# Cross-attention on one core: one reciprocal instruction for two steps' denominators, and a new order of work on all engines

## What is computed

```
xn  = (input - mean) * rsqrt(var + 1e-5) * gamma + beta      # mean and var over the whole sample
q   = Wq @ xn + bq        -> 8 heads of 256 x 64
k,v = Wkv @ context + bkv -> 8 heads of 256 x 64
att = softmax(q k^T / 8)  # 256 x 256 for each head
y   = att @ v
out = input + Wo @ y + bo
```

## Time and profile before

| | us |
|---|---|
| median of 3 runs | 728.08 |
| lowest, highest | 727.77, 731.11 |
| the profiled execution, own time | 729.69 |
| its span, first to last instruction | 727.9 |
| busy DVE, PE, ACT, POOL | 676.4, 670.9, 620.0, 566.5 |
| mean granted clock of TensorE | 0.982 |
| one period of the loop (two samples) | 21.36 and 21.50 in turn |

### The profile page before, as it was taken

One profiled execution on the slowest core, in us unless ns is written; L12 is line 12 of the kernel. 1 busy time (PEld: TensorE's weight loads), 2 busy tenths in 40 slices (PEclk: granted clock), 3 DMA queues, 4 the chain that ended last, 5 costly groups with the idle time before them and its releaser, 6 DMA issues.

```text
span 727.9 us, 29934 instructions
## 1 busy us (share of the span) xinstructions
PE 670.9 (92%) x11204; PEld 445.4 (61%) x11204; DVE 676.4 (93%) x1124; ACT 620.0 (85%) x2248; POOL 566.5 (78%) x360
## 2 busy tenths in 40 slices
PE   5789999999999999999999999999999999899986
PEld 4556666666666656666665666666566666566564
DVE  1599999999999999999999999999999999999992
ACT  2579888899988889988888998888898888899882
POOL 2478888787888878888887888888788888778872
PEclk9789999999999999999999999999999999999997
DMA  6112222222222222222222222222222222222110
GB/s 123 26 53 74 72 57 65 77 70 70 70 72 62 58 69 70 70 74 60 61 67 70 70 70 70 65 58 69 70 70 72 65 66 56 74 73 60 43 47 23
DMA packets 74814, 47.56 MB, mean 65 GB/s; under 512 B 33748, under 2 KB 74708, under 8 KB 74772
## 3 DMA queue, kind: packets, MB, share of 16 engines
q1 hardware_dynamic: 72848, 46.59, 23.9%
q10 hardware_dynamic: 1924, 0.40, 0.3%
HBM read 25.96 MB, written 4.19 MB: 41 GB/s over the span
## 4 chain that ended last, share of the span: by engine, by line
PE 61%; DVE 16%; SPq 9%; issue 7%; ACT 4%; DMA 2%; DVEq 0%; ACTq 0%
PE z L399 30%; PE fill L365 24%; DVE neg_max L536 7%; SPq L290 6%; DVE probs_t L549 6%; PE z L410 4%; ACT probs L481 4%; PE z L424 1%; DVE y L592 1%; PE z L377 1%; DVE spread L580 1%; SPq L253 1%; SPq L242 1%; DMA x_res<-in_x 1%; DMA wv<-in_L_xattn_Wkv 1%
## 5 line engine op out<-in xcount | busy, mean ns | idle before, releaser
L637 POOL TENSOR_TENSOR probs<-probs,recip 128x1024 f32<-128x1024 f32 x256 | 482.1, 1893 | 127.3 <-DVE recip L542 126.3
L481 ACT ACTIVATE probs<-fill,neg_max 128x256 f32<-128x256 f32 x1024 | 472.7, 487 | 76.5 <-DVE neg_max L536 73.1
L536 DVE TENSOR_REDUCE neg_max<-fill 128x4 f32<-128x1024 f32 x256 | 307.8, 1202 | 15.9 <-PE fill L365 14.6
L365 PE MATMUL fill<-c,t 64*128 64x256 f32 x2048 | 290.1, 404 | 32.5 <-ACT probs L481 27.7
L549 DVE STREAM_TRANSPOSE probs_t<-probs 128x1024 f32<-128x1024 f32 x256 | 310.5, 1222 | 3.0 <-POOL probs L637 0.9
L365 PEld LDWEIGHTS fill<-c,t 64*128 64x128 f32 x2048 | 187.4, 189 | 123.6 <-ACT probs L481 88.7
L399 PE MATMUL z<-probs_t,ctx_keys 32*64 32x256 f32 x8192 | 253.1, 380 | 0.8 <-DVE y L592 0.7
L481 ACT ACTIVATION_READ_ACCUMULATOR probs<-fill,neg_max 128x1 f32 x1024 | 224.5, 219 | 0.0
L399 PEld LDWEIGHTS z<-probs_t,ctx_keys 32*64 32x64 f32 x8192 | 175.1, 131 | 64.9 <-issue 35.0
L490 ACT ACTIVATE t<-z,d_col 128x512 f32<-128x512 f32 x128 | 88.5, 740 | 7.4 <-PE z L377 7.4
L497 ACT COPY z_sb<-z 128x1024 f32<-128x1024 f32 x64 | 61.9, 1032 | 7.8 <-PE z L399 7.8
(11 more groups left out here) (38 smaller groups left out, 108.0 us busy)
## 6 DMA issues: line engine op xcount, KB each, us to landing
ctx_keys<-ctx_turned SPq DMA_DIRECT2D x512, 32.0 KB, 1.8
x<-in_x SPq DMA_DIRECT2D x64, 128.0 KB, 2.8
c<-in_ctx SPq DMA_DIRECT2D x64, 128.0 KB, 2.7
ctx_rows<-in_ctx SPq DMA_DIRECT2D x128, 32.0 KB, 1.8
x_res<-in_x SPq DMA_DIRECT2D x32, 128.0 KB, 2.2
out<-y SPq DMA_DIRECT2D x32, 128.0 KB, 1.8
wq<-in_L_xattn_Wq ACTq DMA_DIRECT2D x2, 128.0 KB
wv<-in_L_xattn_Wkv SPq DMA_DIRECT2D x2, 128.0 KB
```

Source lines behind the costliest of these rows:

```text
L365: mm = pe.matmul(banks[:, o, K * qt:K * qt + K], t[p][r:r + 64, hp, s, 128 * qt:128 * qt + 128], c2[p][r:r + 64, s, :], start=True, stop=True)
L481: ins = act.activation(probs[:, k % SLOTS, g, :], bank[:, K * qt:K * qt + K], ACT.Exp, bias=neg_max[:, k, g:g + 1], accum_out=denom[:, k, ...
L536: dve.tensor_reduce(neg_max[:, k, :], fill[k % PAIRS_OF_BANKS][:, :, :].rearrange("p o (t k) -> p (o t) k", t=QT), AX.X, ALU.max, negate=T ...
L637: pool.tensor_tensor(p, p, recip[:, k, :].unsqueeze(2).broadcast_to([128, 2 * QT, K]), ALU.mult).then_inc(probs_ready, 1)
```

## The change

Two things are done together. First, the denominators of steps 2i and 2i+1 are inverted by one instruction over 128 x 8, four times a pair in place of eight times 128 x 4. It waits for the exponentials of both steps, and the divides of both steps wait for it:

```
-            def reciprocal(pair, k):
-                wait(dve, exp_ready, pair.count(UNITS, 2 * k + 2))
-                dve.reciprocal(recip[:, k, :], denom[:, k, :]).then_inc(recip_ready, 1)
+            def reciprocals(pair, i):
+
+                wait(dve, exp_ready, pair.count(UNITS, 4 * i + 4))
+                dve.reciprocal(recip[:, 2 * i:2 * i + 2, :], denom[:, 2 * i:2 * i + 2, :]).then_inc(recip_ready, 1)
...
             def divide(pair, k):
-                wait(pool, recip_ready, pair.count(STEPS, k + 1))
+                wait(pool, recip_ready, pair.count(STEPS // 2, k // 2 + 1))
```

Second, the tables of all engines are replaced:

```
-PE_ORDER = (at('scores', 0.00, 1.20, 3.50, 5.03, 7.25, 10.15, 10.92, 13.57)
-            + at('mix', 18.05, 18.82, 20.27, 21.80, 22.56, 24.01, 24.77, 25.46) + at('project_out', 30.26)
-            + at('project_in', -4.39, -3.70) + at('mean', -16.17) + at('var', -14.90))
-ACT_ORDER = (at('exp', 1.93, 3.30, 5.47, 7.40, 9.19, 12.09, 13.89, 15.69) + at('t', -2.54, -0.74, 1.06, 1.48)
-             + at('z', 26.56, 27.29))
-DVE_ORDER = (at('weights', -2.59, 1.02) + at('max', 0.97, 2.25, 4.51, 6.44, 8.23, 11.13, 12.83, 14.59)
-             + at('recip', 4.45, 6.38, 8.14, 9.07, 10.85, 13.67, 15.43, 18.19)
-             + at('turn', 7.28, 9.13, 9.99, 11.97, 13.73, 15.49, 19.59, 21.35) + at('moments', -28.92)
-             + at('mean_var', -25.79) + at('spread', -15.34) + at('sample_var', -14.19)
-             + at('turn_context', 1.89) + at('result', 32.35))
-POOL_ORDER = (at('divide', 4.65, 6.75, 8.33, 9.74, 11.15, 13.87, 15.63, 18.38) + at('root', -12.21)
-              + at('norm', -14.90, -9.94))
-SYNC_ORDER = (at('load_x', -8.74) + at('load_c', 14.57) + at('load_ct', 2.69) + at('spread_context', 2.49)
-              + at('residual', 24.35) + at('store', 32.85))
+PE_ORDER = (at('scores', 0.00, 1.16, 3.48, 5.68, 7.20, 10.09, 10.85, 13.59)
+            + at('mix', 18.04, 18.80, 20.24, 21.00, 22.44, 23.96, 24.72, 25.40) + at('project_out', 30.27)
+            + at('project_in', -4.47, -3.76) + at('mean', -16.17) + at('var', -15.06))
+ACT_ORDER = (at('exp', 1.90, 3.68, 5.41, 7.61, 9.30, 12.12, 13.90, 15.69) + at('t', -2.52, -0.74, 1.05, 1.47)
+             + at('z', 26.66, 27.39))
+DVE_ORDER = (at('weights', -2.57, 1.01) + at('max', 0.90, 2.73, 4.46, 6.66, 8.35, 11.06, 11.89, 14.51)
+             + at('recip', 5.29, 9.18, 13.59, 17.73)
+             + at('turn', 7.49, 9.75, 12.73, 13.66, 15.35, 17.87, 19.56, 21.36) + at('moments', -22.75)
+             + at('mean_var', -21.39) + at('spread', -15.49) + at('sample_var', -14.20)
+             + at('turn_context', 6.21) + at('result', 32.20))
+POOL_ORDER = (at('divide', 5.49, 6.89, 9.38, 10.78, 13.79, 15.19, 17.93, 19.88) + at('root', -12.67)
+              + at('norm', -15.06, -7.71))
+SYNC_ORDER = (at('load_x', -6.51) + at('load_c', 14.59) + at('load_ct', 7.01) + at('spread_context', 6.81)
+              + at('residual', 24.20) + at('store', 32.70))
```

More of the change, by code:

```diff
@@ L604, in steps @@
                     elif kind == "recip":
-                        reciprocal(owner, item)
+                        reciprocals(owner, item)
                     elif kind == "turn":
```

## The result

The changed kernel takes **829.47 us** (median of 6 runs, 821.47 to 836.96) against 728.13 for the kernel before: ratio 1.134, 95% interval 1.131 to 1.137. The ratio leaves out the two slowest of the six runs (834.17 and 836.96 us), which lie over 1.5% above the fastest and had the lowest granted clocks (0.922 and 0.918). The profiled execution took 828.29 us with a span of 826.5. From the page: the span, busy times, the granted clock in 40 slices, and the chain by engine and by line.

The account below looks back on a forecast made before the run. PE and DVE were taken to bound the old period in turn, SP's transfer queue the new one. 728.08 + 71.2 = 799.3, plus 30.6 us for clock falls, gave 830 us, range 794 to 849.

Parts of the forecast that it names:

- Which ring binds: A closed chain from result through turn_context, SP's issues and the residual replaces the PE and DVE chain: 23.21 us for 21.36.
- a slack of 2.3 us: In the loop before the change, the residual is in at 344.30 and the next result due at 346.61.
- The ring's terms: Result to turn_context 2.17 plus 5.80, first issue 0.47, spread_context 10.22, load_ct 2.31, landing and release 2.24: 23.21 us a period.
- Outside the loop: In about 8 periods around the loop's steady part SP issues slower: 24.94 us, 3.58 more each, plus 1.35 per clock fall.
- The reciprocals: On DVE each costs 0.08 us; only one leaving the chain counts, and that is worth nothing while the transfers bind.
- The wider operand at nothing: Reciprocals on DVE taking 8 elements per partition instead of 4 were costed at no extra time.
- the rival with DVE's queue as the bound: All four dropped reciprocals count, 0.32 us a period, 9.9 less 1.9 at the end: 8 us gained, 720 us; chance 0.04.
- The end: Divide 6 can no longer run under the last exponentials: between 0 and 1.9 us once, taken as 1.9.
- The clock: PE's pauses before var lower TensorE's clock in all 8 long cases and two thirds of 22 others: 30.6 us.
- the step that gave 1.35 us a fall: A low stretch of 3.4 us delays scores 2 before max 2: 1.7 us of PE's work lost, less 0.35 slack.
- The signs: DVE idle before result 1.8 us or more, some 60 in all; PE pause over 2; loop periods 23.2, or 24.6 with falls.
- The ring without falls: Rival: the late residual binds each period but TensorE's clock stays up: 799 us, chance 0.27.

Follow-up runs that it names:

- Experiment 2: Kernel before, reciprocals untouched, with only turn_context, spread_context, load_ct, load_x and the residual moved to where the change has them: 824.46 us, ratio 1.136.
- 3: Changed kernel with turn_context put back early on DVE and SyncE's table as before the change; paired reciprocals stay: 733.83 us, ratio 1.0066.
- experiment 1: Changed kernel with the residual issued at the head of each period, before the 16 transfers of spread_context: 729.86 us, ratio 1.0015.
- 5: Changed kernel with the residual issued behind spread_context's 16 transfers but ahead of load_ct's four: 735.71 us, ratio 1.0085.
- 6: Changed kernel with the residual issued behind load_x too, as the kernel before has it: 906.61 us, ratio 1.240.
- experiment 11: The kernel of experiment 1 with each 128 x 8 reciprocal made by two of 128 x 4 at the same place: 732.64 us, ratio 1.0043.
- experiment 4: Changed kernel with PE making the scores of step 0 three times over, filling its pause before the var sum: 795.25 us, ratio 1.092.

## Why the prediction was right, point by point

- **Which ring binds.** The profile before gave the residual a slack of 2.3 us, and the move took 4.16. Experiment 2 shows that the move is enough, 3 that without it the loss is gone, and 1 that with the residual out of its way it does no harm; 5 and 6 show that the ring's length sets the time.
- **The ring's terms.** 23.21 us forecast, 23.10 in the rows above, 23.06 as a mean. Turns, maxima and reciprocals between result and turn_context summed to 7.97 with what was there; they measured 8.03. Outside the loop: 4.93 us more a period with a fall, forecast; 14.1 / 3 = 4.7 and 17.5 / 4 = 4.4 measured. I counted eight such periods; there are seven, and 2.9 us up to the first result.
- **The reciprocals.** That only those on the chain count is borne out by experiment 11, with the price of two of four. The sizes were too large: start to start the reciprocals of 128 x 4 take 0.06 us as often as 0.08 before the change (medians of 0.056 to 0.079, by what follows). What I overlooked is the one that came in ahead of sample_var (experiment 1), which is the likely reason why against the kernel before nothing was gained, not even with the ring away.
- **The wider operand at nothing.** This term was put at nothing without a measured row of such an instruction, and it takes back about half of what the pairing saves: one of 128 x 8 takes 0.08 to 0.11 us from start to start, so four of them in place of eight narrow ones gain about 0.15 us a period and not 0.32. It hardly moved the forecast, which held these 0.08 us worth nothing while the ring lasts; but the 8 us of the rival with DVE's queue as the bound would have been about 3 (31 x 0.15, less the 1.9 at the end).
- **The end.** 1.9 us for divide 6 was in the sum; the last two periods took 0.3 us more. Turn 7 did come 1.9 us later behind the result (4.46 us against 2.57), and PE paused for it in the middle of the last mix:

```profile
816.02 3.71 PE L399 MATMUL z<-probs_t,ctx_keys 32*64 32x256 f32 x128 [1.41 <-DVE probs_t L550]
```

  The end of the mix came 1.7 us later; but the last project_out then ran at the upper level, in 1.95 us for the 3.02 of the earlier trace rows, which hid 1.1 of it. In experiment 1 it ran at the lower one again, and the last interval was 15.14 us for 12.92.
- **The clock: the total came out right by errors that cancelled, which is luck.** The share of periods with a fall was well guessed: two thirds, and 14 of 22 (64%) in the profiled execution. But the step that gave 1.35 us a fall was mis-sized: it took one low stretch of 3.4 us, all lost work at half speed, less 0.35 of slack. Stretches of 3.4 us cost 1.5, near that; what I left out are the five of 6.8 us, which cost 2.9, and the average is 2.0. Against that, two other terms were too large. The ring's part of a loop period was forecast at 1.85 us, against the shorter of the two old periods, and is 23.06 - 21.43 = 1.63. And outside the loop the ring added about 2.6 us a period where nothing fell (experiment 4), for the 3.58 forecast.

| term, us | forecast | measured |
|---|---|---|
| ring, 22 periods | 40.7 | 35.9 |
| falls in them | 19.8 | 28.0 |
| all outside them | 41.3 | 34.8 |
| sum | 101.8 | 98.6 |

- **The signs.** DVE's idle time before the result came to some 60 us as forecast (62.1), but in the loop it was 1.4 to 1.7 us and not 1.8 or more. PE's pause in the loop was 1.4 to 2.2 us, mostly short of the 2.4, and not over 2 in each period. The periods had three lengths and not two.
- **The rivals.** The ring without falls was put at 799 us; experiment 4, which comes nearest to it, gave 795. By the Trainium skill's page (TensorE: Matmul & The Clock Gate, on HAM oscillation) pauses like these would leave the clock up. The trace disagrees: pauses of 1.57 and 1.59 us were followed by stretches at the lower level. The bound by DVE's queue is out by experiment 11, which has the residual in time and every reciprocal back, and shows 0.08 us a period for the 0.15 that this bound asks for.

## What to carry to other kernels

Before moving a piece of work, write down which transfers are issued behind it, how long the issuing queue takes for each, and what the last of them feeds: here 16 issues of 0.64 us turned a shift of 5.8 us on one engine into a new ring through a queue that no busy table lists. A transfer that nothing delays belongs ahead of such a block. And a pause of 2 us on TensorE can be paid for twice: here it was followed in 14 of 22 periods by 3.4 or 6.8 us at the lower clock.

## What the runs showed of the hardware that I had not expected

- Pauses of nearly the same length had different outcomes: 2.15 us was twice followed by no fall (periods of 22.96 and 22.88 us), 1.57 and 1.59 us by falls, and 1.58 us twice by none. The length of one pause alone doesn't decide it.
- Mix pieces of 32 x 32 blocks, with a weight load for each, follow the clock nearly as the scores do: 3.71 against 1.98 us for 64 records, 1.87 times as long; eight score records take 2.08 against 1.14 us, 1.82 times as long.
